# A gated cross-attention and mixture-of-experts layer: the running maximum of the decay goes through DRAM instead of TensorE

## What is computed

```python
def _mlstm_cell(q, k, v, ...):
    log_f = jax.nn.log_sigmoid(fg)
    cs = jnp.cumsum(log_f, axis=1)
    fg_mat = cs[:, :, None] - cs[:, None, :]
    log_D = jnp.where(mask, fg_mat, -jnp.inf) + ig[:, None, :]
    max_log_D = jnp.max(log_D, axis=-1, keepdims=True)
    D_mat = jnp.exp(log_D - max_log_D)
    C = jnp.einsum('hsd,htd->hst', qh, kh) / np.sqrt(DH) * D_mat
    normalizer = jnp.maximum(jnp.abs(C.sum(axis=-1, keepdims=True)), jnp.exp(-max_log_D))
    h = jnp.einsum('hst,htd->hsd', C / (normalizer + EPS), vh)
...
x = x + tanh(g_xattn) * mlstm(layernorm(x), ctx, ctx)
x = x + tanh(g_ffn) * (experts(layernorm(x)) + shared(layernorm(x)))
```

## Time and profile before

| | |
|---|---|
| median of 3 runs | 1078.76 us (1076.42 to 1082.22) |
| the profiled execution | 1078.9 us, its span 1077.3 us |
| granted TensorE clock, mean | 0.952 |
| PE busy | 960.1 us, 89% of the span |
| DVE busy | 813.8 us, 76% |
| ACT and POOL busy | 424.7 and 423.3 us, 39% each |
| DMA | 147.26 MB |

### The profile page before, as it was taken

How to read it: one execution, slowest core, us unless ns; L and a number is a source line. 1 busy time by engine, 2 the same in 40 slices (tenths; PEclk the granted TensorE clock), 3 DMA queues, 4 the chain that set the end, 5 groups by cost and what they waited for, 6 DMA issues and landing times.

```text
span 1077.3 us, 21069 instructions
## 1 busy us (share of the span) xinstructions
PE 960.1 (89%) x6143; PEld 804.9 (75%) x6143; DVE 813.8 (76%) x1995; ACT 424.7 (39%) x957; POOL 423.3 (39%) x315
## 2 busy tenths in 40 slices
PE   3589999999999998989987199999999999999981
PEld 2479888988888886967777178888888888777761
DVE  2887889888988899888867666666666666655885
ACT  2654445444544455444522034444444444342110
POOL 5010220222022202222123907767767777104775
PEclk9989999999999998989969599999999999999996
DMA  8670211221122112111014455577667675924888
GB/s 256 223 287 2 80 40 40 79 79 40 40 79 79 39 42 79 60 59 41 11 42 159 159 169 179 179 211 212 180 183 228 177 206 155 335 77 149 261 284 263
DMA packets 92778, 147.26 MB, mean 137 GB/s; under 512 B 10720, under 2 KB 51168, under 8 KB 91776
## 3 DMA queue, kind: packets, MB, share of 16 engines
q0 software_dynamic: 17872, 65.02, 18.7%
q1 hardware_dynamic: 60592, 58.74, 17.3%
q10 hardware_dynamic: 14208, 22.16, 5.9%
HBM read 89.26 MB, written 56.62 MB: 135 GB/s over the span
## 4 chain that ended last, share of the span: by engine, by line
PE 69%; DVE 12%; issue 7%; DMA 4%; POOL 4%; ACT 1%; ACTq 1%; SPq 0%; DVEq 0%; POOLq 0%
PE bank L1289 19%; PE bank L1159 13%; PE bank L1308 9%; PE bank L1172 5%; PE bank L1082 4%; PE bank L1014 4%; POOL w_ring L698 3%; PE bank L1103 2%; PE bank L1106 2%; PE bank L1104 2%; PE bank L1356 2%; DMA x2n<-routed_x 2%; PE bank L1132 2%; PE bank L1299 2%; DMA base_out<-in_x_dram 2%
## 5 line engine op out<-in xcount | busy, mean ns | idle before, releaser
L1289 PE MATMUL bank<-w_ring,x2nT 128*128 x948 | 254.0, 406 | 19.9 <-DVE x2nT L1871 19.6
L1289 PEld LDWEIGHTS bank<-w_ring,x2nT 128*128 128x128 f32 x948 | 173.2, 190 | 57.7 <-issue 22.4
L1159 PE MATMUL bank<-x2nT,w_ring 128*128 128x256 f32 x1152 | 149.8, 286 | 0.0
L579 POOL DMA_INDIRECT routed_x<-x2n,slot_u x64 | 68.9, 1077 | 205.6 <-DVE slot_u L1632 190.6
L1159 PEld LDWEIGHTS bank<-x2nT,w_ring 128*128 128x128 f32 x1152 | 142.4, 190 | 0.3
L1308 PE MATMUL bank<-w_ring,sh_actT 128*128 x474 | 121.1, 391 | 3.5 <-DVE sh_actT L1860 3.5
L1860 DVE TENSOR_TENSOR sh_actT<-bank,sh_actT 128x256 fp32r<-128x256 f32 x79 | 33.5, 425 | 108.8 <-ACT sh_actT L929 108.8
L661 POOL TENSOR_TENSOR w_ring<-area,one 128x3072 fp32r<-128x3072 f32 x14 | 74.2, 5303 | 87.3 <-PE bank L1308 87.3
L1308 PEld LDWEIGHTS bank<-w_ring,sh_actT 128*128 128x128 f32 x474 | 88.8, 188 | 24.0 <-issue 4.6
L698 POOL DMA_INDIRECT w_ring<-routed_y,y_slot x64 | 67.8, 1060 | 77.6 <-DMA routed_y<-cs_in 52.6
L664 POOL TENSOR_TENSOR w_ring<-area,w_ring 128x3072 fp32r<-128x3072 f32 x14 | 95.8, 6845 | 2.5 <-POOL w_ring L661 2.5
(11 more groups left out here) (224 smaller groups left out, 1962.0 us busy)
## 6 DMA issues: line engine op xcount, KB each, us to landing
routed_y<-cs_in ACTq DMA_DIRECT2D x79, 256.0 KB, 2.9
x2n<-routed_x SPq DMA_DIRECT2D x300, 64.0 KB, 2.7
base_out<-in_x_dram SPq DMA_DIRECT2D x16, 512.0 KB, 5.1
cs_in<-in_ctx_dram SPq DMA_DIRECT2D x16, 512.0 KB, 4.1
area<-n_L_ffn_expert_gate_dram POOLq DMA_DIRECT2D x16, 512.0 KB, 5.3
area<-in_L_ffn_expert_up_dram POOLq DMA_DIRECT2D x16, 512.0 KB, 6.8
area<-n_L_ffn_expert_down_dram POOLq DMA_DIRECT2D x16, 512.0 KB, 8.4
out_dram<-base_out SPq DMA_DIRECT2D x32, 256.0 KB, 3.9
```

What stands on the lines that cost most here:

```text
L579: pool.indirect_dma_start(out=routed_x, in_=x2n[:, b.par, j, :], in_offset=None, out_offset=bass.IndirectOffsetOnAxis(ap=slot_u[:, b.par, ...
L1159: last = mm(gu_bank(b.n, m)[:, at:at + S], w[:, w_part, c, m * P:(m + 1) * P], x2nT[:, x_part, c, :], start=(c + p == 0), stop=(c == DC - ...
L1289: last = mm(bank[2 + t.par][:, :], xtT[:, x_part, t.par, c * P:(c + 1) * P], w_gu[:, bass.ds(slot, 1), w_part, c, :].rearrange("p a i -> p ...
```

## The change

max_row is stored to DRAM (max_rows, 8 KB per batch) by SP. For each pair of heads SP then loads it back with a stride of zero over partitions: 256 queries for each head (256 KB), and the last 128 once more (128 KB), into max_spread, which has room for two pairs. POOL's `mask` fills the entries above the diagonal with one affine_select of 128x512 per pair, and ACT's `head` reads SBUF. The spreads on PE, the bf16 parts and their constants are gone, and with them ACT's copy and three DVE operations per batch. The four banks now all belong to scores: pairs 0 and 1 stand together at the begin of a step, pairs 2 and 3 together after the first transpose of x. DVE's scan waits until the maxima of the batch before have been stored. Between steps and tiles three things move: SP loads the first four tiles too, in place of ACT; DVE does the last shared addition before it splits expert 0; POOL waits for that split before it begins with expert 1.

```diff
+    max_rows = nc.dram_tensor("max_rows", (2, NH, S), F32).ap()
...
-        TP, SM, MB, QK, HO, FF = bank[0], bank[1], bank[2:4], bank[4:6], bank[6], bank[7]
+        TP, SM, QK, HO, FF = bank[0], bank[1], (bank[4:6], bank[2:4]), bank[6], bank[7]
...
-        head_sel = sb("head_sel", [P, NH, P], BF16)
...
-        max_rest = sb("max_rest", [FG + NH, S])[FG:, :]
-        max_parts = sb("max_parts", [P, 2, S], BF16)
+        max_spread = sb("max_spread", [P, 2, 2 * ST + 2, P])
...
+            def max_store(b):
+                sp.wait_ge(row_step.sem, row_step.upto(b.n, 4))
+                sp.dma_start(max_rows[b.par], max_row[:, :]).then_inc(max_out.sem, 16)
+            def max_load(b, q):
+                k, lap = q % 2, b.n * 2 + q // 2
+                sp.wait_ge(max_out.sem, max_out.upto(b.n))
+                sp.wait_ge(decay_made.sem, decay_made.upto(b.n, 2 * q - 2))
+                two = max_rows[b.par, 2 * q:2 * q + 2, :]
+                sp.dma_start(max_spread[:, k, 0:2 * ST, :].rearrange("p (h j) n -> p h (j n)", h=2),
+                             two.partition_broadcast(P)).then_inc(max_in[k].sem, 16)
+                sp.dma_start(max_spread[:, k, 2 * ST:, :], two[:, P:S].partition_broadcast(P)
+                             ).then_inc(max_in[k].sem, 16)
+            def max_front(b):
+                max_store(b)
+                max_load(b, 0)
+                max_load(b, 1)
+            def max_back(b):
+                max_load(b, 2)
+                max_load(b, 3)
             load_next(Item(0, 2))
+            max_front(Item(0, 0))
+            max_back(Item(0, 0))
             load_next(Item(0, 3))
             sp.wait_ge(zeros_made.sem, zeros_made.upto(0))
             sp.dma_start(routed_x[0:DUMP, :].rearrange("(e r) d -> r e d", e=E)[0:P],
                          zeros.unsqueeze(1).to_broadcast([P, E, D])).then_inc(padded.sem, 16)
             sp.dma_start(routed_x[DUMP:DUMP + P, :], zeros).then_inc(padded.sem, 16)
+            max_front(Item(0, 1))
             sp.wait_ge(shared_in.sem, shared_in.upto(SHARED_PIECES - 1))
             for part in range(2):
                 sp.dma_start(kept_w[part], sh_flat[:, part, :].bitcast(F32)).then_inc(kept_w_out.sem, 16)
             for b in range(4, B):
...
                     sp.wait_ge(padded.sem, padded.upto(1))
+                max_back(Item(0, b - 3))
                 load_next(Item(0, b), more=b + 2 < B)
+                max_front(Item(0, b - 2))
+            for b in range(B - 3, B):
+                max_back(Item(0, b))
+                if b + 1 < B:
+                    max_front(Item(0, b + 1))
...
-            for n in range(XRING, TILES):
-                sp.wait_ge(xt_turned.sem, xt_turned.upto(n - XRING))
+            for n in range(TILES):
+                if n >= XRING:
+                    sp.wait_ge(xt_turned.sem, xt_turned.upto(n - XRING))
...
+            def mask(b, q):
+                k, lap = q % 2, b.n * 2 + q // 2
+                pool.wait_ge(max_in[k].sem, max_in[k].upto(lap))
+                own = max_spread[:, k, 0:2 * ST, :]
+                g.affine_select(out=own, in_=own, compare_op=ALU.is_ge, fill=MASK, base=0,
+                                pattern=[[0, 2 * ST], [1, P]], channel_multiplier=-1).then_inc(max_masked.sem, 1)
...
                 N, F, A, G, H = t + 2, t + 1, t, t + -1, t + -2
                 if route:
                     h_stats(G)
+                if attend:
+                    mask(A, 2)
+                    mask(A, 3)
+                if front:
+                    values(F)
                 if route:
                     x2_stats(G)
+                if ahead:
+                    stats(N)
+                if front:
+                    mask(F, 0)
+                    mask(F, 1)
                 if rest and route:
                     scatter(H)
-                if front:
-                    values(F)
-                if ahead:
-                    stats(N)
...
             def drain(G, H):
...
             pool.wait_ge(sh_down_made.sem, sh_down_made.upto(SH[LAST]))
             pool.wait_ge(kept_w_out.sem, kept_w_out.upto(1))
             pool.wait_ge(expert_dma[1].sem, expert_dma[1].upto(0))
+            pool.wait_ge(expert_in.sem, expert_in.upto(0))
             g.tensor_tensor(w_ring[:, 1, 0, :], stage[1], one[:, :].to_broadcast([P, EW]), ALU.mult).then_inc(expert_hi_in.sem, 1)
             pool.wait_ge(expert_hi_in.sem, expert_hi_in.upto(0))
-            pool.wait_ge(expert_in.sem, expert_in.upto(0))
             g.tensor_tensor(w_ring[:, 1, 1, :], stage[1], w_ring[:, 1, 0, :], ALU.subtract
                             ).then_inc(expert_in.sem, 1)
             load_expert(2, 0)
...
-            def max_hi(b):
-                act.wait_ge(row_step.sem, row_step.upto(b.n, 4))
-                act.wait_ge(max_spread.sem, max_spread.upto(b.n - 2))
-                s.copy(max_parts[0:NH, b.par, :], max_row[:, :]).then_inc(max_hi_made.sem, 1)
...
             def head(b, h):
...
-                act.wait_ge(max_spread.sem, max_spread.upto(b.n, h + 1))
+                act.wait_ge(max_masked.sem, max_masked.upto(b.n * 4 + h // 2))
...
-                s.activation(decay[:, k, 0:S], MB[k][:, 0:S], ACT.Exp,
+                s.activation(decay[:, k, 0:S].rearrange("p (j n) -> p j n", j=ST),
+                             max_spread[:, h // 2 % 2, k * ST::2 * ST - k, :], ACT.Exp,
...
-                s.activation(decay[:, k, S:TRI], MB[k][:, S:TRI], ACT.Exp,
+                s.activation(decay[:, k, S:TRI], max_spread[:, h // 2 % 2, k * ST + 1, :], ACT.Exp,
...
-            act.wait_ge(tables_made.sem, tables_made.upto(0))
-            for par in range(2):
-                act.wait_ge(scattered[par].sem, scattered[par].upto(B // 2 - 1))
-            for n in range(XRING):
-                row = act.value_load(row_tab[0:1, n:n + 1], min_val=0, max_val=DUMP)
-                load_rows(act, row, n)
...
-                pe.wait_ge(c_made.sem, c_made.upto(b.n, 2 * q))
+                pe.wait_ge(c_made.sem, c_made.upto(b.n, 2 * q - 2))
...
-                        last = mm(QK[k][:, at:at + n], ctxT[half, b.par, q, frm:frm + P],
+                        last = mm(QK[q % 2][k][:, at:at + n], ctxT[half, b.par, q, frm:frm + P],
...
-            def spread(b, h):
-                k = h % 2
-                pe.wait_ge(row_step.sem, row_step.upto(b.n))
-                pe.wait_ge(decay_made.sem, decay_made.upto(b.n, h - 1))
-                for at, n in ((0, S), (S, P)):
-                    mm(MB[k][:, at:at + n], head_sel[0:3 * FG, h, :], max_parts[0:3 * FG, b.par, S - n:S],
-                       start=True, stop=False)
-                    last = mm(MB[k][:, at:at + P], identb[:, :], mask_b[:, :], start=False, stop=True)
-                last.then_inc(max_spread.sem, 1)
...
                 mix = route and G.n in SH
                 if attend:
                     scores_pair(A, 0)
-                    spread(A, 0)
-                    spread(A, 1)
+                    scores_pair(A, 1)
                 if rest:
                     shared(H, 2)
                 if front:
                     turn_ctx(F, 0)
                 if attend:
-                    spread(A, 2)
-                    spread(A, 3)
                     pv(A, 0)
                     pv(A, 1)
-                    scores_pair(A, 1)
                 if front:
                     turn_ctx(F, 1)
                 if rest:
...
                 if front:
                     turn_x(F, 0)
                 if attend:
-                    spread(A, 4)
-                    spread(A, 5)
                     scores_pair(A, 2)
+                    scores_pair(A, 3)
                 if front:
                     turn_x(F, 1)
                 if attend:
...
                     pv(A, 3)
                 if front:
                     gates_pe(F)
-                if attend:
-                    spread(A, 6)
-                    spread(A, 7)
                 if front:
                     gates_sum(F)
                 if route:
...
                     turn(G, 1, front)
                 if rest:
                     shared_down(H, 1)
-                if attend:
-                    scores_pair(A, 3)
                 if route:
                     router(G, front)
                 if mix:
...
+                dve.wait_ge(max_out.sem, max_out.upto(b.n - 1))
...
-                dve.wait_ge(max_hi_made.sem, max_hi_made.upto(b.n))
-                v.tensor_tensor(max_rest[:, :], max_row[:, :], max_parts[0:NH, b.par, :], ALU.subtract
-                                ).then_inc(row_step.sem, 1)
-                dve.wait_ge(row_step.sem, row_step.upto(b.n, 6))
-                v.tensor_copy(max_parts[FG:FG + NH, b.par, :], max_rest[:, :]).then_inc(row_step.sem, 1)
-                dve.wait_ge(row_step.sem, row_step.upto(b.n, 7))
-                v.tensor_tensor(max_parts[2 * FG:2 * FG + NH, b.par, :], max_rest[:, :],
```

(9 more changed lines are left out.)

38 lines of the change are left out of this document (13 added, 25 removed).

## The result

The changed kernel takes 1105.4 us in the median of 4 runs (1103.43 to 1109.2), the kernel before 1077.61 in the runs beside it: a ratio of 1.0244, with a 95% interval of 1.0205 to 1.0283. The direction was forecast, the size was not: +27.8 us instead of +6, and outside the range. The profiled span grows from 1077.3 to 1101.8 us.

A forecast was written before the change was run, and what follows sets the result against it. DVE was taken to set the pace in most of a full step, PE late only at its two ends. 1078.9 + 14 + 0.1 - 3 - 5.5 = 1084.5, rounded to 1085 us; range 1064 to 1100.

The forecast's parts named there:

- The start: Batches 0 and 1: the way through DRAM and loads held behind kept_w cost +14 us, bounds +3 and +16.
- the late steps: Steps without shared expert: DVE's waits for pair 1's scores mostly vanish, 4 us; in sum -3, bounds -6 and +3.
- The way through DRAM: Store, loads and mask, 6.2 us: hidden in full steps, 3.1 in each of batches 0 and 1, 0.4 per late step.
- Rival A: Start: batch 1's loads are not held by kept_w, costing 3 instead of 14, 1074 or 1067 us; chance 0.28.
- The full steps: Eight repeated steps: 0.9 lost against 0.89 gained in each, flat at +0.1 us, bounds -7 and +10.5.
- the wait of 0.39 at the transpose: Full step, at 244.78: DVE's wait of 0.39 us for a transpose of PE can vanish.
- the step's end: End of a full step: PE reaches the shared matmuls in time, worth 0.50 us.
- The term that was mis-sized is the collisions: Full steps: GpSimd's masks and value copy beside DVE's additions cost 0.9 us a step, bounds nothing and 2.2.
- Rival C: Full steps: all collisions are paid in full, 2.2 us a step, +10.5 on the forecast, 1095 us; chance 0.12.
- Rival B: Full steps: emptier PE falls to 1.2 GHz, 1.9 us a step, +15 over eight steps, 1100 us; chance 0.15.
- The tail: Between steps and tiles: scatter saves 3 us, loads leave ACT free, first expert matmul earlier; -5.5 us, bounds -8 and -3.

The follow-up runs named there:

- e2: Changed kernel with the zero fill in four and kept_w in six pieces of about 1 MB, placed between or behind loads of maxima, same queue; 1087.51 us, ratio 1.0044.
- e1: Changed kernel with the store and loads of batch 1's maxima issued by ACT, in another DMA queue than the large transfers; 1107.97 us, ratio 1.0214.
- e4: Changed kernel with 40 unused bf16 128x128 matmuls per batch put on PE ahead of the scores; 1116.59 us, ratio 1.0303.
- e5: Changed kernel with POOL's scatter moved behind the first power of the following step; 1104.23 us, ratio 1.0229.
- e6: Changed kernel whose loads read constant maxima and go out ahead of the store, real maxima left out of the result; 1090.75 us, ratio 1.0101.
- e7: Changed kernel with the constant maxima of e6 and without POOL's masks as well; 1085.66 us, ratio 1.0056.
- e9: Changed kernel with 24 unused matmuls ahead of the first x2 transpose and 24 ahead of the router, in the steps to scans 12 and 14; 1104.74 us, ratio 1.0210.

## Why the prediction was wrong, point by point

**The start** was the right mechanism with the wrong size: +14 forecast, +24.8 measured, above the bound of +16. Alone it would have given 1084.5 + 10.8 = 1095.3, past the forecast's own 1076 to 1093 and inside 1064 to 1100; with the late steps on top the time leaves that range too. The failing step is "its loads go out a landing and a mask earlier (2.9 + 0.55), at 62, and kept_w right behind them". It gave batch 1's store the price of an idle queue, and let only the later loads meet a large transfer. The chain has 8.32 us for that store, since the zero fill was under way. The zero fill in turn was issued 10.3 us later than before (50.38 against 40.12), because the context load ahead of it on SP waits for the value copy and the copy for masks, a link that the prediction did not follow. So loads went out at 66.64, kept_w at 68.49, pairs 2 and 3 landed at 90 instead of 78 to 81, and the normalization came at 93.51 instead of 84. The way through DRAM in batches 0 and 1 cost 7.0 by e2, against 3.1 twice in the sum. Of the rule used, that a load waits for a large transfer ahead, "of the same queue" was too narrow: e1 shows a wait of 19 us from another queue. Rival A, that the loads pass kept_w, is out.

**The full steps**: flat forecast, -2.4 measured, within the bounds. The gain was 0.89 at most in the text and is 0.8 by e4. It is made up otherwise than said: the wait of 0.39 at the transpose is gone, but the step's end gives 0.13 instead of 0.50 (first silu product 5.02 us behind the scan instead of 5.15), since PE there now waits for DVE's L1651; the rest lies in smaller gaps. The term that was mis-sized is the collisions: 0.9 in the sum, while the step shown has 0.37, at L1535, which was named as a place for them. The Trainium skill's rule on the shared ports (page "SBUF — State Buffer", section "SBUF: two separate sides") agrees with these rows: L1535 has two tiles in SBUF, and the first of its two operations delays the mask, which takes 0.82, before the mask delays the second. With one SBUF tile, L1493 of e5 waits as well, so two inputs are not the only case here; whether that one ran in the two-port mode that this page of the Trainium skill names too, no row tells. Rival C, all collisions in full with 2.2 a step, is out. Rival B as priced, the half clock in every full step, is out: the granted clock is 1.00 in the eight steps from scan 3 to scan 11.

**The late steps**: -3 forecast, +6.5 measured, the other term outside its bounds. DVE's waits for the scores of pair 1 did vanish as said (4.3 us). The failing step is the way through DRAM, "about even with the time there is" and priced at 0.4 for each of three steps. It looked at the exponentials alone. On POOL the masks that wait for the loads hold back the scatter and the power behind them, and DVE waits 4.8 us for that power. Without the way and the masks 10.2 us of this stretch go away (e6, e7), more than the 6.5 that were lost. Rival B's mechanism, at a place where it was not looked for, may add to it: e9 shows the low clock reaching into the steps to scans 13 and 15 (3.6 us), but the filled steps lost as much, so its share stays open.

**The tail**: -5.5 forecast, -4.75 in the changed kernel and -6.0 alone, from the cast to the first expert matmul. The scatter is not held up (0.96 instead of 4.08), and the loads leave ACT free. Right.

With the measured sizes the prediction's own sum reads 1078.9 + 24.8 - 2.4 + 6.5 - 4.75 + 0.3 = 1103.4, the time of the profiled execution; the stretches leave nothing out.

## What to carry to other kernels

Before a small transfer is put on the path, list which large transfers are under way at each of its occurrences, the first ones above all, and follow what moves the large ones themselves: here an 8 KB store took 8.32 us and loads 15.32 us. Another queue was no remedy; putting the large transfers behind the small ones, in pieces of 1 MB, gave back 17.8 of 24.8 us, and 10.6 came from moving kept_w alone, uncut. Where DVE sets the pace of a stage, 2.2 us less of PE were worth 0.8, and one addition that met the new work on POOL took 0.37 of that back. On an engine that works in order, look at what stands behind a new wait: here the power behind the masks.

## What the runs showed of the hardware that I had not expected

Loads of 384 KB a pair, issued by ACT while SP's kept_w was under way, kept their reader waiting for 19 us: the DMA engines moved 112 packets of either queue in 6 us, and those of SP were 12 times as large. POOL's copy and selections lengthened single DVE operations by 0.4 to 0.8 us, tiny ones too (0.95 instead of 0.16 for 128x16); where they fell changed when the masks were taken away, and the step became 0.37 us longer. The low clock behind a gap of PE outlasted the step in which the gap stood (0.63 over the first 6 us of the next one, 1.00 with the gaps filled).
